# Attention and top-k experts on one core: fetching each expert's tokens by indirect DMA instead of a 0/1 matrix product

## The reference

```
x = L0_attn_x                                   # 16 batches, 256 tokens, 128 channels, f32
x = x + attention(layernorm(x))                 # 16 heads, key width 8, value width 64, causal
xn = layernorm(x)
probs = softmax(xn @ gate_w)                    # 8 experts
top_p, top_idx = top_k(probs per batch and expert, 64)
xin = xn[top_idx]                               # 64 tokens for each batch and expert
h = gelu(xin @ w1[e]);  y = (h @ w2[e]) * top_p # 128 -> 512 -> 128
out = x + scatter_add(y at top_idx)
```

## Time and profile before

| | |
|---|---|
| median of 3 runs | 593.4 us (592.84 to 594.67) |
| the profiled execution: time | 594.03 us |
| the profiled execution: span | 592.3 us |
| granted TensorE clock, mean | 0.973 of full speed |
| PE busy | 531.8 us (90%) |
| DVE / ACT / POOL busy | 406.4 / 394.4 / 259.2 us |
| DMA queue of SP and ACT | 44.73 MB in 49040 packets |

### The profile page before, as it was taken

How to read it: one execution, slowest core, us unless ns; L and a number is a source line. 1 busy time by engine, 2 the same in 40 slices (tenths; PEclk the granted TensorE clock), 3 DMA queues, 4 the chain that set the end, 5 groups by cost and what they waited for, 6 DMA issues and landing times. The chain is left out here.

```text
span 592.3 us, 14090 instructions
## 1 busy us (share of the span) xinstructions
PE 531.8 (90%) x4773; PEld 428.9 (72%) x4773; DVE 406.4 (69%) x1014; ACT 394.4 (67%) x1370; POOL 259.2 (44%) x247
## 2 busy tenths in 40 slices
PE   1389999999999999999999999997149999999996
PEld 1257777777777777777777777775028989989895
DVE  4377888888888888888888887864763234433344
ACT  2288989888989888888898898971215443343230
POOL 7255565555565655565655555561600110110111
PEclk9989999999999999999999999999569999999999
DMA  4975152251341422522514315500021001000001
GB/s 123 241 207 189 37 139 74 73 143 46 99 130 29 124 77 65 142 66 76 141 29 115 97 45 143 144 1 1 1 61 30 20 19 37 20 11 19 19 20 45
DMA packets 49659, 45.82 MB, mean 77 GB/s; under 512 B 4176, under 2 KB 46416, under 8 KB 49616
## 3 DMA queue, kind: packets, MB, share of 16 engines
q1 hardware_dynamic: 49040, 44.73, 27.7%
q10 hardware_dynamic: 576, 0.52, 0.3%
HBM read 26.35 MB, written 18.89 MB: 76 GB/s over the span
## 5 line engine op out<-in xcount | busy, mean ns | idle before, releaser
L367 ACT ACTIVATE prob<-s_ps,neg_max 128x128 f32<-128x128 f32 (+1 forms) x512 | 210.1, 439 | 24.5 <-DVE neg_max L523 22.8
L351 POOL TENSOR_TENSOR probn<-prob,inv 128x1024 f32<-128x1024 f32 x64 | 121.2, 1894 | 45.0 <-DVE inv L527 45.0
L367 ACT ACTIVATION_READ_ACCUMULATOR prob<-s_ps,neg_max 128x1 f32 x512 | 115.2, 225 | 0.0
L344 POOL TENSOR_TENSOR probn<-prob,inv 128x512 f32<-128x512 f32 x64 | 66.6, 1040 | 90.6 <-PE t_ps L640 79.2
L618 PE MATMUL ctx_ps<-probT,v_sb 128*64 128x256 f32 (+1 forms) x1024 | 97.3, 332 | 0.6 <-issue 0.6
L618 PEld LDWEIGHTS ctx_ps<-probT,v_sb 128*64 128x64 f32 x1024 | 63.5, 136 | 27.7 <-issue 9.1
L807 POOL TENSOR_TENSOR y_parts<-y_sb,y_parts 128x512 fp32r<-128x512 f32 x16 | 20.6, 1285 | 137.1 <-ACT y_parts L823 137.1
L454 DVE TENSOR_REDUCE neg_max<-s_ps 128x4 f32<-128x1024 f32 x64 | 76.5, 1196 | 1.0 <-PE s_ps L556 1.0
L631 PE MATMUL misc_ps<-wo_sb,ctxT 128*128 128x128 f32 x512 | 73.9, 288 | 0.0
L631 PEld LDWEIGHTS misc_ps<-wo_sb,ctxT 128*128 128x128 f32 x512 | 61.9, 191 | 10.8 <-issue 10.8
L580 PE MATMUL t_ps<-ident,probn 128*128 128x128 f32 x256 | 62.5, 284 | 1.0 <-ACT probT L404 0.6
(11 more groups left out here) (146 smaller groups left out, 1044.0 us busy)
## 6 DMA issues: line engine op xcount, KB each, us to landing
qT<-q_rows SPq DMA_DIRECT2D x16, 512.0 KB, 4.0
q_rows<-qk_hi SPq DMA_DIRECT2D x32, 128.0 KB, 2.4
q_rows<-qk_lo SPq DMA_DIRECT2D x32, 128.0 KB, 2.4
k_diag_even<-k_rows SPq DMA_DIRECT2D x32, 128.0 KB, 4.2
k_diag_odd<-k_rows SPq DMA_DIRECT2D x32, 128.0 KB, 4.3
k_rows<-qk_hi SPq DMA_DIRECT2D x30, 128.0 KB, 2.4
k_rows<-qk_lo SPq DMA_DIRECT2D x30, 128.0 KB, 2.4
w_raw<-in_L_ffn_w SPq DMA_DIRECT2D x1, 2048.0 KB, 10.6
```

The costliest lines, as they stand in the source:

```text
L344: nc.gpsimd.tensor_tensor(probn[r][:, 0:HG * P].rearrange("p (i k) -> p i k", i=HG), prob[r][:, 0:HG * P].rearrange("p (i k) -> p i k", i=HG),
L351: nc.gpsimd.tensor_tensor(probn[r][:, HG * P:].rearrange("p (i k) -> p i k", i=HG), prob[r][:, HG * P:].rearrange("p (i k) -> p i k", i=HG ...
L367: last = nc.scalar.activation(prob[r][:, first + i * keys:first + (i + 1) * keys], scores[:, i, :], ACT.Exp, bias=neg_max[:, r, block_, i: ...
```

## The change

Tokens are no longer picked by a product. Instead:

- In attention, `xg_hi` and `xg_lo` (ScalarE and VectorE, 16 each) are gone. SyncE stores `xn2` of each batch as 256 rows of 512 bytes in a DRAM tensor `xn2_rows` (`store_tokens`): for batch b - 4 at the head of SyncE's turn for batch b, for the last batches behind the load of w2. VectorE may overwrite `xn2` only when the store before has landed (`xn2_stored`), and SyncE ends the stage when all have.
- `tok_row`, its way through DRAM, `toks`, `pick` and the pick products are gone. VectorE adds 256 x batch to `slot_tok` (`slot_row`), and GpSimd issues four indirect DMAs for each unit (`gathers`): each fetches the 128 rows (64 for each expert of the pair) of one batch to one part of `xs`, which is a ring of three units.
- TensorE turns the four parts of a unit by four 128x128 transposes into one PSUM tile `xin_ps`; ScalarE copies it to `xin_hi`, VectorE subtracts it for `xin_lo`. This is done for unit n + 1 at the head of step n.
- The loop runs from -1 to 17. PSUM that the picks used serves the last batches' sums; two more `place` buffers serve the last two batches.

```diff
@@ attention, SyncE
+            def store_tokens(b):
+                sp.wait_ge(xn2_ready, b + 1)
+                sp.dma_start(xn2_rows[b * T:(b + 1) * T, :].rearrange("(t p) d -> p t d", p=P),
+                             xn2[:, :, :]).then_inc(xn2_stored, 16)
             for b in range(B):
+                if b >= 4:
+                    store_tokens(b - 4)
...
+            store_tokens(B - 4)
             sp.wait_ge(s1_done, G * (B - 1))
             sp.dma_start(w2_sb[:, :, :, :], w2.rearrange("e (k p) c -> p e k c", p=P)).then_inc(experts_loaded, 16)
+            for b in range(B - 3, B):
+                store_tokens(b)
+            sp.wait_ge(xn2_stored, 16 * B)
@@ attention, ScalarE, VectorE
-                        nc.scalar.activation(xg_hi[:, bass.ds((b - 2) * TB, TB), :], xn2[:, :, :],
-                                             ACT.Copy).then_inc(xg_hi_done, 1)
-                        await_count(dve, xg_lo_done, b - 2)
+                        await_count(dve, xn2_stored, (b - 2) * 16)
-                        nc.vector.tensor_tensor(xg_lo[:, tiles, :], xn2[:, :, :], f32(xg_hi[:, tiles, :]),
-                                                ALU.subtract).then_inc(xg_lo_done, 1)
@@ experts, GpSimd
+            def gathers(n):
+                if has(n, B):
+                    await_count(pool, xin_done, n - GATHERS + 1)
+                    for q in range(QB):
+                        b = n // QB * QB + q
+                        nc.gpsimd.indirect_dma_start(
+                            xs[n % GATHERS][:, q, :], None, xn2_rows,
+                            bass.IndirectOffsetOnAxis(ap=slot_row[:, n % EP, b:b + 1], axis=0)).then_inc(gathered[n % GATHERS], 16)
+            pool.wait_ge(xn2_stored, 16 * B)
+            pool.wait_ge(rows_ready, 1)
+            for n in range(GATHERS):
+                gathers(n)
             for m in range(B):
+                gathers(m + GATHERS)
                 parts = y_parts[m // QB % RING]
                 pool.wait_ge(y_hi_ready, m + 1)
                 nc.gpsimd.tensor_tensor(parts[:, :, m % EP, 1, :], y_sb[m % RING][:, :, :],
@@ experts, VectorE
+            nc.vector.tensor_tensor(slot_row[:, :, :], slot_tok[:, :, :], row_base[:, :, :], ALU.add).then_inc(rows_ready, 1)
+                    nc.vector.tensor_tensor(xin_lo[w % RING][:, :, :, :], xin_ps[:, :, :].rearrange("p b (h s) -> p h b s", h=2),
+                                            f32(xin_hi[w % RING][:, :, :, :]), ALU.subtract).then_inc(xin_lo_ready, 1)
@@ experts, TensorE
+                w = n + 1
+                if has(w, B):
+                    pe.wait_ge(gathered[w % GATHERS], 16 * QB * (w // GATHERS + 1))
+                    await_count(pe, xin_lo_ready, w)
+                    for q in range(QB):
+                        last = nc.tensor.transpose(xin_ps[:, q, :], xs[w % GATHERS][:, q, :], ident[:, :])
+                    last.then_inc(xin_done, 1)
```

More of the change, by code:

```diff
@@ L672, in _, with experts @@
             batches(pe, batch)
-def experts(nc, out_tiles, x_all, xg_hi, xg_lo, gate_logit, ident, w1_raw, w2_sb, experts_loaded):
+def experts(nc, out_tiles, x_all, xn2_rows, gate_logit, ident, w1_raw, w2_sb, experts_loaded, xn2_stored):
     with ExitStack() as ctx:
@@ L693, in experts @@
         QB = 4
-        LB = 2
-        LOADS = B // LB
-        STEPS = range(-4, B + 2)
+        GATHERS = 3
+        STEPS = range(-1, B + 2)
         LAST = B - QB
@@ L713, in experts @@
         slot_prob = sb("slot_prob", [P, EP, B])
-        tok_no = sb("tok_no", [P, TB])
+        row_base = sb("row_base", [P, EP, B])
+        slot_row = sb("slot_row", [P, EP, B], U32)
         col_no = sb("col_no", [P, T], BF16)
[L716 to L719, removed]
+        xs = [sb(f"xs{r}", [P, QB, D]) for r in range(GATHERS)]
+        xin_hi = [sb(f"xin_hi{r}", [P, 2, QB, CAP], F32R) for r in range(RING)]
+        xin_lo = [sb(f"xin_lo{r}", [P, 2, QB, CAP], F32R) for r in range(RING)]
         hT = [w1_raw[:, r * EP:(r + 1) * EP, :].rearrange("p (h a) (k n) -> p h (a k) n", h=2, n=QB * CAP)
@@ L723, in experts @@
         y_parts = [sb(f"y_parts{r}", [P, QB, EP, 2, D], F32R) for r in range(RING)]
[L724 to L728, removed]
+        place = [sb(f"place{r}", [P, EP, T], F32R) for r in range(2 * RING)]
+        xin_ps = ps("xin_ps", [P, QB, 2 * CAP])
         h_ps = [ps(f"h_ps{r}", [P, 2, QB * CAP]) for r in range(RING)]
@@ L731, in experts @@
         out_ps = ps("out_ps", [P, TB, 2, D])
-        last_place = [part[:, :, :].rearrange("p t (a n) -> p (t a) n", a=2) for part in pick]
-        last_out_ps = [to[:, :, :].rearrange("p (t a e) s -> p t a (e s)", t=TB, a=2)
-                       for to in (*pick_hi_ps, *pick_lo_ps)]
+        last_ps = [ps(f"last_ps{i}", [P, TB, 2, D]) for i in range(QB - 1)]
         def out_ps_of(b):
-            return out_ps[:, :, :, :] if b < LAST else last_out_ps[b - LAST]
+            if b < LAST:
+                return out_ps[:, :, :, :]
+            if b < B - 1:
+                return last_ps[b - LAST][:, :, :, :]
+            return xin_ps[:, :, :].rearrange("p (t a) d -> p t a d", t=TB)
         def place_of(b):
-            return place[b % RING][:, :, :] if b < B - RING else last_place[b % RING]
+            return place[b % RING if b < B - RING else b % RING + RING][:, :, :]
         numbered = sem("numbered")
@@ L749, in experts @@
         found = sem("found")
-        row_ready = sem("row_ready")
-        row_stored = sem("row_stored")
-        toks_loaded = [sem(f"toks_loaded{i}") for i in range(LOADS)]
+        rows_ready = sem("rows_ready")
+        gathered = [sem(f"gathered{r}") for r in range(GATHERS)]
         twice_ready = sem("twice_ready")
@@ L757, in experts @@
         w1_ready = sem("w1_ready")
[L758 to L759 removed]
+        xin_done = sem("xin_done")
         xin_hi_ready = sem("xin_hi_ready")
@@ L777, in _ @@
         def _(sp):
[L778 to L785, removed]
             with sp.Fori(0, B) as b:
@@ L826, in _ @@
             for n in STEPS:
[L827 to L831, removed]
+                w = n + 1
+                if has(w, B):
+                    act.wait_ge(xin_done, w + 1)
+                    await_count(act, h_done, 4 * (w - 1))
+                    nc.scalar.activation(xin_hi[w % RING][:, :, :, :], xin_ps[:, :, :].rearrange("p b (h s) -> p h b s", h=2),
                                          ACT.Copy).then_inc(xin_hi_ready, 1)
@@ L889, in _ @@
             dve.wait_ge(numbered, 2)
[L891 to L900, removed]
+            dve.wait_ge(slots_ready, 2)
+            nc.vector.tensor_tensor(slot_row[:, :, :], slot_tok[:, :, :], row_base[:, :, :], ALU.add).then_inc(rows_ready, 1)
             def placing(b):
```

44 lines of the change are left out of this document (15 added, 29 removed).

## The result

The changed kernel takes **630.81 us** (median of 4 runs, 629.62 to 632.97) beside 594.03 for the kernel before (4 runs, 592.84 to 594.69): a ratio of 1.062, with a 95% interval from 1.059 to 1.066. It is slower by 6%. The profiled execution has a span of 627.9 us, 35.6 more than before.

The account below looks back on a forecast made before the run. TensorE bounds the kernel, but GpSimd's late gathers would set the expert steps' period: +24.6 for twelve periods, +0.45 for step 14, +1.1 for the head, +26.1 on 594.03, 620.1, less 0.6 to the median: 619.5 us; range 597 to 646.

Parts of the forecast that it names:

- The period's sum, the term that decides: Steps 2 to 14: GpSimd's 4.5 to subtraction's end, four issues of 1.1, landing 1.9 give 10.8 us a step; +24.6 us.
- The clock, left to a rival: Rival for the expert steps: every stall drops TensorE to half speed, period 12.2 us, 636 us in all; chance 0.22.
- the prediction's single step of 8.26 us: TensorE's own need for a full expert step once the pick is replaced by four transposes, 0.6 us shorter than before.
- The head: From the indices through the first steps: eight issues delay h to 445.7; with low clock and step 1's gain, +1.1 us.
- The low clock: In the head, only transposes precede h, so TensorE starts it slow; charged 1.0 us, between 0 and 1.4.
- the faster rival: Rival: gather issues on GpSimd are cheap (0.48 us) and hidden, period 7.9 below TensorE's 8.26; 586 us, chance 0.10.
- What costs nothing: Attention: removing xg_hi and xg_lo gives 0; the xn2 stores land in 2.4 us, only the last could show, at most 0.5.
- An issue of 1.9: Rival: a gather's issue costs GpSimd 1.89 us, period 14.0, 664 us; chance 0.15 for an issue above 1.3.
- step 14 onward: End of the expert steps: step 14 has its transposes as well, +0.45 us; behind it nothing changes in length.

Follow-up runs that it names:

- two kernels that break one link each: Against the changed kernel: gathers issued one place earlier in GpSimd's order, 592.62 us; transposes of unit n + 1 moved behind h of step n, 594.25 us.
- 1.3 us of filling: Changed kernel plus 12 idle transposes of the identity on TensorE at the head of steps 3 to 14, during the gather wait; 627.23 us.

## Why the prediction was right

The direction and the mechanism were right, and 630.8 lies in the range of 597 to 646; the forecast of 619.5 was 11 us low, a loss of 26.1 foreseen against 35.6 in the profile.

- **The period's sum, the term that decides.** Its form was right in every part: the gathers begin right behind the subtraction, TensorE waits for them once at the head of each of steps 3 to 14 (30.1 us, 2.5 each in the mean, as forecast) and never at the head of steps 1 and 2, and two kernels that break one link each lose the whole wait. In numbers, at full clock: start to end of subtraction 4.6 (541.12 to 545.71; 4.5 was taken), from there to the transposes 6.5 (6.3 was taken). 11.1 in place of 10.8, 3.6 us over twelve steps. That the 6.3 came so near is in part luck, since the two unknown prices erred in opposite directions: an issue is 1.25 apart, not 1.1 (0.6 more, with 0.15 ahead of the first), and the landing is 2.5 to 2.6 from the *start* of the last issue, where I had laid 1.9 behind its end, 3.0 in all (0.4 less).
- **The clock, left to a rival.** This is the step that was mis-sized. The rival said that each stall brings the clock down and the period goes to 12.2, 636 us, chance 0.22; the forecast had no such term for the steps. Six of twelve periods were longer than 11.6, by 6.1 us together beyond 11.1. The term was wanting, and the rival's "every stall" was too much: half-way between forecast and rival, 628, would have been near, but nothing in the rows of before said half. What the prediction's single step of 8.26 us hid is that the stalls are unequal. With a period that GpSimd sets, a step without *out* (2 to 4) leaves a long wait behind it, 3.2 to 3.7 us, and a step in which *out* waits for the subtraction (5, 9, 13) a short one, 1.5 to 1.6. Of the seven waits of 2.65 us and more, six went with a fall of the clock; of the five up to 2.14, none did. Three of them (steps 4, 9 and 13; a wait that met a fall, and two that did not):

```profile
481.63 0.66 PE L968 MATMUL xin_ps<-ident,xs 128*128 128x128 f32 x4 [3.72 <-DMA xs<-xn_rows,slot_row]
...
541.12 0.66 PE L968 MATMUL xin_ps<-ident,xs 128*128 128x128 f32 x4 [2.14 <-DMA xs<-xn_rows,slot_row]
...
586.10 0.66 PE L968 MATMUL xin_ps<-ident,xs 128*128 128x128 f32 x4 [2.71 <-DMA xs<-xn_rows,slot_row]
```

- **The head.** From the indices (432.33) to the transposes of step 2 it took 25.7 us; 434.1 to 458.35, 24.25, was forecast. The transposes of unit 1 come 12.4 us behind the indices, where 10.7 was summed: 0.9 more by GpSimd's start (first issue at 433.19), 1.3 more by the spacing, 0.5 less by the landing. The low clock cost about what was charged: *h* started at 445.46, most of its first twelve products are listed with 0.41 us in place of 0.28, and the clock rose at 448. The Trainium skill (DMA: Bandwidth & Descriptors, Anatomy of one DMA — SWDGE path) had most of a fixed 2 us in completion and little in generation. For the rows the run with half of them agrees (0.04 us for 64), and landing at 2.5 us is near; but the fixed 1.2 us between issues is not in that section, and the time that I gave by its split, that of the faster rival, did not come.
- **What costs nothing.** Right: attention's busy share is unchanged, and its length from batch 2 on is the same to 0.14 us. The 1.8 us by which it ended earlier came from its first 45 us and from its last six, as shown above. The stores of `xn2` did not land in the 2.4 us that I took from stores of the same size: the first thirteen took 4.4 in the median, the last three 1.8 (last section). The only one that could show, the last, is one of the fast ones: issued at 412.12, landed at 413.92, just ahead of the last gate logits (413.90 to 414.07). With the 4.4 of the first ones it would have landed at 416.5 and held the stage up by more than 2 us (an estimate from these numbers), so that this term came to nothing rests on a landing that the prediction did not foresee.
- **The rivals.** Issues cheap enough to hide needed 0.55 us; they are 1.25. An issue of 1.9 was as far off. The twelve steps and step 14 onward add up: 26.1 + 9.6 (twelve periods: 139.2 for 129.6) + 1.4 (head) - 1.8 (attention's spread) + 0.3 = 35.6.

Was the idea good otherwise? Freed of the wait, with the gathers one place earlier, the steps take 100.6 in place of 105.0: 4.4 us is what the transposes save TensorE. The further 1.7 us, to 98.9, come with the subtraction on VectorE, which shortens the steps in which *out* waits for it (9.5 to 8.9 us). The head takes 2.4 us more (iota to the transposes of step 2: 43.6 against 41.1), since eight issues of 1.25 us stand between the indices and the first *h*.

## What to carry to other kernels

A ring of n buffers gives a lead of n only if the engine that issues the loads is not held, in its own order, by something that comes late in the step before the one that needs them: write the period as "start to what holds the issuer, plus issues, plus landing" and compare it with the step. Moving a load one place up in the issuer's order, or its consumer behind work that is ready, won back 38 and 37 us here, with no more memory. A wait that is added to TensorE is to be priced with its clock: about a fifth on top of the wait here (6.1 on 30.1 us). Look at each wait and not at their mean: it was the long ones that met a falling clock.

## What the hardware showed that I had not expected

- An indirect DMA holds GpSimd for a fixed time: 1.21 us from one issue to the next with 64 rows, 1.25 with 128. So of the two sizes measured 128 rows are the cheaper by far for each row, and eight issues in a row delay the first use by 10 us.
- Stalls of nearly one length can differ in what the clock does: of four waits of 2.65 to 2.71 us in the changed kernel three met a fall and one (step 13) did not. With 1.3 us of filling ahead of the rest of the wait, the waits left were 2.3 us at most; the two longest (2.09 and 2.27) met a fall, those of up to 1.6 did not.
- One and the same store, 128 KB in rows of 512 bytes into `xn2_rows`, landed in 4.4 us or in 1.8. The first thirteen (window 80 to 370 us) were issued while SyncE's five loads of queries and keys, issued just ahead, had not landed; the last three (375 to 420) had none in flight:

```profile
xn_rows<-xn SPq DMA_DIRECT2D x13, 128.0 KB, 4.4
...
xn_rows<-xn SPq DMA_DIRECT2D x3, 128.0 KB, 1.8
```

The median of all sixteen, 4.2, against the 2.4 of the query rows, looks like a price of the short rows; the last three, with the same rows, show that it isn't. That the loads in flight are the cause was not tested by itself.
